# A recommendation tower on one core: one-hot results evicted in pairs, id spreads by DMA, and the moves of one tile spread among Gram units

## The chip, the cores and the metric

The kernel runs on one core of a Trainium2 chip. The metric is the device time of one execution in microseconds, 122.56 us before the change (median of three runs, 122.13 to 122.66). The engines are named as the profile names them: PE is TensorE (PEld its weight load), DVE is VectorE, ACT is ScalarE, POOL is GpSimd, SP is SyncE. The source writes `scalar` for ACT and `vector` for DVE.

## The reference

A batch of 512 rows. Each row has a dense feature vector (128 numbers) and 26 ids; each id picks a row of 128 numbers from its own table. The 27 vectors of a row are multiplied pairwise, and the 351 products go with the dense vector, twice, into a small network.

```python
e = jnp.stack([tbl_0[ids[:, 0]], ..., tbl_25[ids[:, 25]]], axis=1)            # 512 x 26 x 128
combined = jnp.concatenate([dense[:, None, :], e], axis=1)                     # 512 x 27 x 128
interactions = jnp.einsum('bfd,bgd->bfg', combined, combined)                  # 27 x 27 per row
z = jnp.concatenate([dense, interactions[:, iu, ju]], axis=1)                  # upper triangle, 351
h = jnp.concatenate([z, dense], axis=1)                                        # 607
h = jnp.maximum(h @ W_top1 + b_top1, 0.0)                                      # 512
h = jnp.maximum(h @ W_top2 + b_top2, 0.0)                                      # 256
y = h @ W_top3                                                                 # 1
```

Ten of the 26 tables have 1000 rows; the others have 1250 to 125000.

## The kernel before, in words

All engines walk one list, `STEPS`, which `plan_steps` writes out by hand (L110 to L144). Each engine takes its own part of each step, in the order of the list, and waits on semaphores for the others. So the list sets the order on PE, DVE and ACT; SP and POOL have fixed orders of their own.

**One-hot stage.** The ten tables of 1000 rows are loaded whole (SP, L264) and looked up by a product. For table `i`, PE spreads its 512 ids over the partitions (`bcast`, L540): two products of 128x512, one into the PSUM region `gram[0]` that DVE reads, one into `gram[1]` that ACT reads. DVE and ACT then write the one-hot matrix in eight chunks of 128 rows (`mark`): in each half of four chunks DVE does three by a comparison (L460), ACT one by two activations (L396, L400). The table is split into two parts so that the product is exact enough: ACT rounds it (`cast`, L386) and DVE forms what is left (`low`, L452). PE multiplies, 16 products a table (`onehot`, L561), into one of four PSUM banks that are used in a ring (`RING`). ACT copies each result bank into `xT` (L434), which holds for each batch row its 27 vectors plus five of them a second time (32 slots of 4 bytes side by side). The dense vectors are turned by PE (`dense`, L549) and copied by ACT three times: into `denseT` and into two slots that are not neighbours.

**Gathered tables.** The other 16 tables are fetched row by row by POOL: 64 indirect DMAs (L305), 16 for each of four batch tiles of 128 rows, in groups of four. After some groups POOL waits until the first three gathers of a group have landed. For each group PE does four transposes (`group`, L572) and ACT or DVE copies the bank into `xT`.

**Tail.** For each batch tile PE forms the pairwise products four batch rows at a time (`gram`, L587), in four units of eight, which alternate between the regions `gram[0]` and `gram[1]`. Each unit is staged: ACT copies one half of the columns (L410), DVE overlays the others through masks (L473, L476). After the fourth unit the *moves*, eight copies of 32x96 on ACT (L417) and eight on DVE (L484), bring the staged products into `pairs`. Then come the first layer in two halves (L601, L603), ACT and DVE each taking one half out of PSUM, the second layer (L615), and on DVE the third (L502, L506). A last product turns the 512 results into rows (L620).

PE, before the first real product, runs transposes that only keep it busy: `WARM_UP` (L528) and `FILL` (L545).

## Time and profile before

| what | us |
|---|---|
| median of the runs (three) | 122.56 |
| the profiled execution itself | 122.37 |
| its span | 120.6 |
| PE busy (685 products) | 111.4 |
| DVE busy | 79.6 |
| ACT busy | 71.7 |
| POOL busy | 67.2 |
| last one-hot product ends at | 57.8 |
| last gather issued at | 93.0 |

The span is the time from the first to the last instruction in the profile; the execution's own time is 1.77 us longer. PE's granted clock is 1.00 of full speed in every stretch. A busy time of PE is not PE at its peak, because products are pipelined; where the start times of neighbouring rows tell more than the durations, they are used. In the chain of waits each piece starts where the one before it ends.

### The profile page before, as it was taken

How to read it: one execution, taken by the hardware profiler on the slowest of the kernel's cores; microseconds unless marked ns; L12 is line 12 of the kernel's file. 1: busy time of each engine (PE TensorE's matmuls, PEld its weight loads, DVE VectorE, ACT ScalarE, POOL GpSimd, SP SyncE). 2: the span in 40 equal slices, each digit the busy share in tenths (PEclk: the TensorE clock that was granted, in tenths of full speed). 3: DMA queues.
4: the chain of work that ended last, by engine and by line, in shares of the span. 5: the costliest groups of instructions: out<-in, count | busy, mean ns of one | idle time of the engine just before them, and what ended most of it. 6: DMA issues, size and time to landing. Idle time of an engine off the chain costs nothing.

```text
span 120.6 us, 1879 instructions
## 1 busy us (share of the span) xinstructions
PE 111.4 (92%) x685; PEld 94.1 (78%) x685; DVE 79.6 (66%) x128; ACT 71.7 (59%) x132; POOL 67.2 (56%) x72
## 2 busy tenths in 40 slices
PE   4979999999999999999799949999999879998981
PEld 4647776866867768688699949989999769998960
DVE  1359999999999999991035762892439822564231
ACT  0399499999999999994531641680336522255200
POOL 3777477747688688677767477767767100000000
PEclk9999999999999999999999999999999999999999
DMA  3993755270643978212111112112211100000000
GB/s 64 389 370 115 232 203 177 84 222 23 217 137 126 235 285 302 56 44 58 50 44 50 45 50 60 45 44 63 52 44 49 38 0 5 0 0 0 0 0 1
DMA packets 4964, 11.99 MB, mean 99 GB/s; under 512 B 1742, under 2 KB 2002, under 8 KB 4956
## 3 DMA queue, kind: packets, MB, share of 16 engines
q1 hardware_dynamic: 2888, 7.67, 19.0%
q0 software_dynamic: 2048, 4.20, 12.3%
q8 instruction: 5, 0.08, 0.3%
q10 hardware_dynamic: 20, 0.02, 0.1%
q14 instruction: 3, 0.02, 0.1%
HBM read 11.88 MB, written 0.00 MB: 99 GB/s over the span
## 4 chain that ended last, share of the span: by engine, by line
PE 80%; ACT 11%; DVE 4%; issue 2%; POOL 0%; POOLq 0%; ACTq 0%; DVEq 0%
PE bank L561 32%; PE gram L587 21%; PE bank L615 6%; PE bank L572 6%; PE gram L540 5%; ACT pairs L417 5%; PE bank L603 4%; ACT xT L434 2%; DVE stage L473 2%; PE bank L528 2%; PE bank L601 2%; ACT stage L410 2%; ACT L396 1%; DVE stage L476 1%; DVE parts L452 1%
## 5 line engine op out<-in xcount | busy, mean ns | idle before, releaser
L305 POOL DMA_INDIRECT gath<-in_tbl,idx x64 | 66.3, 1036 | 26.0 <-issue 16.2
L561 PE MATMUL bank<-onehot,parts 128*128 128x512 f32 x160 | 41.0, 411 | 0.7 <-DVE parts L452 0.7
L561 PEld LDWEIGHTS bank<-onehot,parts 128*128 128x128 f32 x160 | 30.7, 197 | 8.0 <-issue 1.7
L460 DVE TENSOR_TENSOR onehot<-gram,row 128x1536 fp32r<-128x1536 f32 x20 | 34.6, 1746 | 2.1 <-PE gram L540 2.1
L587 PE MATMUL gram<-xT 128*128 128x108 f32 x256 | 29.5, 276 | 3.0 <-DVE stage L476 1.6
L587 PEld LDWEIGHTS gram<-xT 128*128 128x128 f32 x256 | 29.0, 192 | 3.7 <-ACT xT L434 1.9
L473 DVE COPY_PREDICATED stage<-overlaid,gram 128x384 f32<-128x384 int32 x16 | 9.3, 582 | 22.6 <-ACT stage L410 22.6
L434 ACT COPY xT<-bank 128x512 f32<-128x512 f32 x22 | 19.5, 920 | 5.4 <-PE bank L572 3.1
L410 ACT COPY stage<-gram 128x384 f32<-128x384 f32 x16 | 7.6, 480 | 22.5 <-PE gram L587 22.5
L396 ACT ACTIVATE distance<-gram,minus_row 128x512 f32<-128x512 f32 x20 | 13.6, 678 | 0.0
L452 DVE TENSOR_TENSOR parts<-table,parts 128x1024 fp32r<-128x1024 f32 (+1 forms) x11 | 12.3, 1117 | 1.6 <-ACT parts L386 1.6
L603 PE MATMUL bank<-pairs,wp 128*128 128x128 f32 x96 | 13.3, 275 | 0.0
L400 ACT ACTIVATE onehot<-distance 128x512 fp32r<-128x512 f32 x20 | 12.6, 632 | 0.6
L603 PEld LDWEIGHTS bank<-pairs,wp 128*128 128x128 f32 x96 | 12.0, 192 | 0.0
L386 ACT CAST parts<-table 128x1024 fp32r<-128x1024 f32 (+1 forms) x11 | 10.5, 961 | 1.6 <-PE bank L561 1.6
L417 ACT COPY pairs<-stage 32x96 f32<-32x96 f32 x32 | 8.6, 268 | 4.2 <-DVE stage L476 3.9
L572 PE MATMUL bank<-ident,gath 128*128 128x128 f32 x64 | 9.5, 279 | 0.5 <-ACT xT L434 0.5
L572 PEld LDWEIGHTS bank<-ident,gath 128*128 128x128 f32 x64 | 7.1, 141 | 3.4 <-issue 2.2
L540 PE MATMUL gram<-ids_r,pick 10*128 10x512 f32 x20 | 8.2, 493 | 0.0
L484 DVE COPY pairs<-stage 32x96 f32<-32x96 f32 x32 | 7.8, 243 | 0.6
L615 PE MATMUL bank<-w_sb,h1T 128*128 128x256 f32 x32 | 7.7, 385 | 0.0
L601 PE MATMUL bank<-denseT,wd 128*128 128x128 f32 x32 | 6.3, 278 | 0.4 <-ACT pairs L417 0.4
(32 smaller groups left out, 47.8 us busy)
## 6 DMA issues: line engine op xcount, KB each, us to landing
table<-in_tbl SPq DMA_DIRECT2D x10, 512.0 KB, 3.3
gath<-in_tbl,idx POOLq DMA_INDIRECT x64, 2.6
wp<-in_w_pairs SPq DMA_DIRECT2D x1, 768.0 KB, 7.1
w_sb<-in_w SPq DMA_DIRECT2D x1, 512.0 KB, 7.6
dense_sb<-in_dense SPq DMA_DIRECT2D x1, 256.0 KB, 4.7
wd<-in_w_dense_a SPq DMA_DIRECT2D x1, 256.0 KB, 6.0
wd<-in_w_dense_b SPq DMA_DIRECT2D x1, 256.0 KB, 6.7
b_bc<-in_b SPq DMA_DIRECT2D x1, 128.0 KB, 7.5
```

What stands on the lines that cost most here:

```text
L305: nc.gpsimd.indirect_dma_start(gath[:, t % GATHER_TILES, s, :], None, tables[GATHERED[s]], bass.IndirectOffsetOnAxis(idx[:, t * TABLES + G ...
L396: nc.scalar.activation(distance[:, n % 2, :], bcast_bank(i, "scalar"), ACT.Abs, bias=minus_row[:, c:c + 1]).then_inc(distance_ready, 1)
L417: last = nc.scalar.copy(dst, src)
L434: last = nc.scalar.copy(dst, src)
L452: nc.vector.tensor_tensor(parts[:, i % 2, 1, c], table[:, i % 3, c], parts[:, i % 2, 0, c].bitcast(F32), ALU.subtract).then_inc(parts_read ...
L460: nc.vector.tensor_tensor(onehot[:, i % 2, c, :], bcast_bank(i, "vector").unsqueeze(1).broadcast_to([P, len(chunks), BATCH]), row[:, c].un ...
L540: last = nc.tensor.matmul(bcast_bank(i, engine), pick[:, i:i + 1].broadcast_to([NOH, P]), ids_r[:], start=True, stop=True)
L561: last = nc.tensor.matmul(dst[:], parts[:, i % 2, part, c * DIM:(c + 1) * DIM], onehot[:, i % 2, c, :], start=(c == 0 and part == 0), stop ...
L572: last = nc.tensor.transpose(dst[:, n * P:(n + 1) * P], gath[:, t % GATHER_TILES, slot, :], ident[:])
L587: last = nc.tensor.matmul(gram[region][:, q, 0:4 * FEATURES], quad, quad[:, :, 0:FEATURES], start=True, stop=True)
L603: last = nc.tensor.matmul(to, wp[:, r, h], pairs[:, t % 2, r, :], start=False, stop=(r == BLOCKS - 1))
L615: last = nc.tensor.matmul(dst[:, 0:H2], h1T[:, t % 2, c, :], w2_sb[:, c, :], start=(c == 0), stop=(c == H1 // P - 1))
```

## The change

The batch rows of a tile are renumbered on the host (ids and dense alike), so that a result bank is copied in the order in which `xT` lies. Then:

- **Pairs.** Two one-hot results lie in two neighbouring banks, and one ACT copy (`pair`) takes both, two neighbouring slots at a time: 128x512x2 elements. The last pair is split, half of the batch on ACT, half on DVE (`pair_rest`).
- **Dense.** The dense vectors come by DMA already turned (`denseT`, `dense_qj`); one ACT copy writes them into two neighbouring slots. PE's four transposes and three ACT copies go.
- **Ids.** ACT's spread of ids for tables 2 to 9 comes by DMA (`spread_ids`, 256 KB written each), in SP's queue. PE does one spread product a table instead of two. The spreads of tables 0 and 1 are done at once, before `FILL`; `WARM_UP` goes from 9 to 7. ACT loads its function table at the very start (a one-column activation), and its first cast goes ahead of its first mark.
- **Groups.** Only tile 0's four groups stand in the one-hot stage, in banks of the region `gram[1]`, and ACT copies them. Tile 1's four groups stand between the first Gram units. The last tile is gathered into `table`, which is free by then, and its last group is copied in two halves (`group_rest`).
- **Tail.** `moves` is a step of its own: tile 0's moves stand between tile 1's Gram units in three pieces, tile 1's and 2's after their units, tile 3's after its own. `sum`, the DVE addition for the dense weights, moves from the one-hot stage to behind tile 0's Gram units. Tile 2's first layer stands ahead of tile 3's Gram units, around the last group; tile 2's second layer behind them.

The core of the diff:

```diff
-GROUPS = [list(range(g, min(g + GROUP, NG))) for g in range(0, NG, GROUP)]
+GROUPS = [list(range(g, g + GROUP)) for g in (NG - GROUP, *range(0, NG - GROUP, GROUP))]
 RING = 4
-GROUP_BEHIND = {1: 1, 2: 1, 3: 1, 4: 1, 6: 1, 7: 1, 8: 1, 9: 1}
-WARM_UP = 9
+GROUP_BEHIND = {1: 1, 3: 1, 5: 1, 7: 1}
+WARM_UP = 7
 HALVES = 2
 SPREAD_REGION = {"vector": 0, "scalar": 1}
...
-    steps = [("bcast", 0), ("mark", 0, 0), ("cast", 0, 0), ("low", 0, 0), ("mark", 0, 1), ("cast", 0, 1), ("low", 0, 1)]
-    steps += [("cast", 1, 0), ("bcast", 1), ("mark", 1, 0), ("low", 1, 0), ("mark", 1, 1)]
+    steps = [("bcast", 0), ("bcast", 1), ("fill",), ("cast", 0, 0), ("mark", 0, 0), ("low", 0, 0), ("cast", 0, 1), ("mark", 0, 1), ("low", 0, 1)]
+    steps += [("cast", 1, 0), ("mark", 1, 0), ("low", 1, 0), ("mark", 1, 1)]
...
-    steps += take(1, 2 * len(GROUPS)) + grams(0) + grams(1)
-    steps += layer1(0) + take(2, 4) + [("layer2", 0)] + grams(2)
-    steps += take(3, 2) + layer1(1) + take(3, 1) + [("layer2", 1)] + take(3, 1) + grams(3)
-    steps += layer1(2) + [("layer1", 3, 0), ("layer2", 2), ("layer1", 3, 1), ("layer2", 3)]
-    return steps + [("turn",)]
+    steps += gram(0, 0) + take(2) + gram(0, 1) + take(1) + gram(0, 2) + take(1) + gram(0, 3) + [("sum",)]
+    steps += gram(1, 0) + moves(0, [0, 1]) + gram(1, 1) + moves(0, [2]) + gram(1, 2) + moves(0, [3]) + gram(1, 3)
+    steps += moves(1) + layer1(0) + take(4) + [("layer2", 0)] + grams(2)
+    steps += take(2) + moves(2) + layer1(1) + take(1) + [("layer2", 1), ("layer1", 2, 0)] + take(1)
+    steps += [("group_rest", *steps[-1][1:]), ("layer1", 2, 1)] + grams(3) + moves(3)
+    return steps + [("layer2", 2)] + layer1(3) + [("layer2", 3), ("turn",)]
...
+            def spread_ids(i):
+                if i >= SCALAR_SPREADS + 2:
+                    sp.wait_ge(onehots_ready["scalar"], HALVES * SCALAR_CHUNKS * (i - 1))
+                sp.dma_start(ids_bc[:, i % 2, :], ids_rows[i:i + 1, :].broadcast_to([P, BATCH])
+                             ).then_inc(ids_bc_loaded[i], 16)
+
             load_table(0)
             load_table(1)
-            sp.dma_start(dense_sb[:], dense).then_inc(dense_loaded, 16)
+            spread_ids(2)
             load_table(2)
+            sp.dma_start(dense_qj[:], dense_qj_t).then_inc(dense_qj_loaded, 16)
+            for i in range(3, NOH):
+                load_table(i)
+                spread_ids(i)
+            sp.dma_start(denseT[:], dense_t).then_inc(denseT_loaded, 16)
             sp.dma_start(wd[:, 0, :], w_dense_a).then_inc(wd_loaded, 16)
             sp.dma_start(wd[:, 1, :], w_dense_b).then_inc(wd_loaded, 16)
-            for i in range(3, NOH):
-                load_table(i)
             sp.dma_start(overlaid[:], masks).then_inc(masks_loaded, 16)
             sp.dma_start(wp[:], w_pairs).then_inc(wp_loaded, 16)
...
+        def pair_slots(s, first_tile, tiles):
+
+            first = 2 * s[1]
+            n = slice(first_tile * P, (first_tile + tiles) * P)
+            return (xT[:, first_tile:first_tile + tiles, :, :, first:first + 2].rearrange("p t q j s -> p (t q j) s"),
...
+                elif s[0] == "dense":
+                    act.wait_ge(dense_qj_loaded, 16)
+                    nc.scalar.copy(xT[:, :, :, :, DENSE_SLOT:DENSE_SLOT + 2].rearrange("p t q j s -> p (t q j) s"),
+                                   dense_qj[:].unsqueeze(2).broadcast_to([P, BATCH, 2])).then_inc(freed["scalar"], 1)
+                elif s[0] == "pair":
+                    act.wait_ge(bank_full, USE[("onehot", 2 * s[1] + 1)] + 1)
+                    dst, src = pair_slots(s, 0, TILES // 2 if s == LAST_PAIR else TILES)
+                    nc.scalar.copy(dst, src).then_inc(freed["scalar"], 1)
```

On ACT, one table of the one-hot stage, with a group's copy behind it. Before (a cast, the copy of a result, two marks, a group's copy); `bank2` and `bank3` are result banks:

```order
L386 CAST parts<-table 128x1024 [waits bank_full,table_loaded5]
L434 COPY xT<-bank2 128x4x4x32 [waits bank_full]
L396 ACTIVATE distance<-gram1,minus_row 128x512 [waits onehots_by_scalar,bcast_full]
L400 ACTIVATE onehot<-distance 128x512 [waits distance_ready]
L396 ACTIVATE distance<-gram1,minus_row 128x512 [waits onehots_by_scalar]
L400 ACTIVATE onehot<-distance 128x512 [waits distance_ready]
L434 COPY xT<-bank3 128x128x4 [waits bank_full]
```

Now, for a table with a pair:

```order
L464 CAST parts<-table 128x1024 [waits bank_full,table_loaded7]
L521 COPY xT<-bank0 128x512x2 [waits bank_full]
L477 ACTIVATE distance<-ids_bc,minus_row 128x512 [waits onehots_by_scalar,ids_bc_loaded7]
L481 ACTIVATE onehot<-distance 128x512 [waits distance_ready]
L477 ACTIVATE distance<-ids_bc,minus_row 128x512 [waits onehots_by_scalar]
L481 ACTIVATE onehot<-distance 128x512 [waits distance_ready]
L524 COPY xT<-gram1 128x128x4 [waits bank_full]
```

The copy of a result is twice as long and comes with every second table; the ids are read from `ids_bc`, and ACT waits for a DMA there, not for PE; the group's bank lies in `gram1`.

On PE, from the end of the one-hot stage into the Gram units. Before (tile 0's units; all groups of tiles 0 and 1 are done):

```order
L587 MATMUL gram0<-xT 128x108 [waits freed_by_vector,freed_by_scalar]
L587 MATMUL gram0<-xT 128x108 x7
L587 MATMUL gram1<-xT 128x108 x8
L587 MATMUL gram0<-xT 128x108 [waits staged]
L587 MATMUL gram0<-xT 128x108 x7
L587 MATMUL gram1<-xT 128x108 [waits staged]
L587 MATMUL gram1<-xT 128x108 x7
L587 MATMUL gram0<-xT 128x108 [waits staged,freed_by_vector,freed_by_scalar]
L587 MATMUL gram0<-xT 128x108 x7
L587 MATMUL gram1<-xT 128x108 [waits staged]
```

Now tile 1's groups (`gath`) stand between tile 0's units:

```order
L692 MATMUL gram0<-xT 128x108 [waits freed_by_scalar]
L692 MATMUL gram0<-xT 128x108 x7
L680 MATMUL bank1<-ident,gath 128x128 [waits last_row_in1_0,rows_in1_0,freed_by_scalar]
L680 MATMUL bank1<-ident,gath 128x128 x3
L680 MATMUL bank1<-ident,gath 128x128 [waits last_row_in1_1,rows_in1_1,freed_by_scalar]
L680 MATMUL bank1<-ident,gath 128x128 x3
L692 MATMUL gram1<-xT 128x108 [waits freed_by_scalar]
L692 MATMUL gram1<-xT 128x108 x7
L680 MATMUL bank0<-ident,gath 128x128 [waits last_row_in1_2,rows_in1_2,freed_by_vector]
L680 MATMUL bank0<-ident,gath 128x128 x3
L692 MATMUL gram0<-xT 128x108 [waits staged,freed_by_scalar]
L692 MATMUL gram0<-xT 128x108 x7
```

The groups moved from the one-hot stage to here, and every unit has its own wait for the copies into `xT`.

On PE, from the last group of gathered rows (`rows_in3_3`). Before:

```order
L572 MATMUL bank0<-ident,gath 128x128 [waits rows_in3_3,last_row_in3_3,freed_by_vector,freed_by_scalar]
L572 MATMUL bank0<-ident,gath 128x128 x3
L587 MATMUL gram0<-xT 128x108 [waits staged,freed_by_vector,freed_by_scalar]
L587 MATMUL gram0<-xT 128x108 x7
L587 MATMUL gram1<-xT 128x108 [waits staged]
L587 MATMUL gram1<-xT 128x108 x7
L587 MATMUL gram0<-xT 128x108 [waits staged]
L587 MATMUL gram0<-xT 128x108 x7
L587 MATMUL gram1<-xT 128x108 [waits staged]
L587 MATMUL gram1<-xT 128x108 x7
L601 MATMUL bank1<-denseT,wd 128x128 [waits moved_by_scalar,moved_by_vector,freed_by_vector,freed_by_scalar]
```

Now:

```order
L680 MATMUL bank0<-ident,table 128x128 [waits last_row_in3_3,rows_in3_3,freed_by_vector]
L680 MATMUL bank0<-ident,table 128x128 x3
L706 MATMUL bank0<-denseT,wd 128x128 [waits moved_by_vector,moved_by_scalar,freed_by_vector]
L708 MATMUL bank0<-pairs,wp 128x128 x3
L706 MATMUL bank0<-denseT,wd 128x128
L708 MATMUL bank0<-pairs,wp 128x128 x3
L692 MATMUL gram0<-xT 128x108 [waits staged,freed_by_vector,freed_by_scalar]
L692 MATMUL gram0<-xT 128x108 x7
```

and, two units later:

```order
L692 MATMUL gram1<-xT 128x108 [waits staged,freed_by_vector,freed_by_scalar]
L692 MATMUL gram1<-xT 128x108 x7
L720 MATMUL bank1<-w2_sb,h1T 128x256 [waits freed_by_scalar,freed_by_vector]
L720 MATMUL bank1<-w2_sb,h1T 128x256
L720 MATMUL bank1<-w2_sb,h1T 128x256 [waits freed_by_vector]
L720 MATMUL bank1<-w2_sb,h1T 128x256
L706 MATMUL bank1<-denseT,wd 128x128 [waits moved_by_vector,moved_by_scalar,freed_by_scalar]
L708 MATMUL bank1<-pairs,wp 128x128 x3
```

Half a first layer (of tile 2) now stands between the last group and the Gram units of tile 3, and a second layer alone, where before there were a whole first layer and more, between those units and the first layer of tile 3.

## Rows read from the trace of the kernel before

**Rows 1.** The page: busy times; the gathers (busy, mean ns); table loads (median us to landing).

```profile
PE 111.4 (92%) x685; PEld 94.1 (78%) x685; DVE 79.6 (66%) x128; ACT 71.7 (59%) x132; POOL 67.2 (56%) x72
...
L305 POOL DMA_INDIRECT gath<-in_tbl,idx x64 | 66.3, 1036 | 26.0 <-issue 16.2
...
table<-in_tbl SPq DMA_DIRECT2D x10, 512.0 KB, 3.3
```

**Rows 2.** Chain of waits, start and one-hot stage: start us, us, what.

```profile
1.52 2.18 PE bank L528 x9
...
4.94 1.28 ACT L396
...
20.96 3.66 PE bank L561 x16
24.62 0.65 PE gram L540 x2
```

**Rows 3.** Timeline of TensorE, first one-hot product: start us, us, instructions [idle before].

```profile
8.98 5.84 PE L561 MATMUL bank<-onehot,parts 128*128 128x512 f32 x16 [0.65 <-DVE parts L452]
```

**Rows 4.** Timeline of VectorE, one-hot stage and one block of moves.

```profile
17.19 1.22 DVE L452 TENSOR_TENSOR parts<-table,parts 128x1024 fp32r<-128x1024 f32 x1
...
19.98 0.68 DVE L515 TENSOR_TENSOR wd<-wd 128x512 f32<-128x512 f32 x1
...
33.86 3.40 DVE L460 TENSOR_TENSOR onehot<-gram,row 128x1536 fp32r<-128x1536 f32 x2
...
38.33 3.44 DVE L460 TENSOR_TENSOR onehot<-gram,row 128x1536 fp32r<-128x1536 f32 x2
...
91.40 2.03 DVE L484 COPY pairs<-stage 32x96 f32<-32x96 f32 x8
```

**Rows 5.** Timeline of ScalarE, one table of the one-hot stage.

```profile
30.68 1.04 ACT L386 CAST parts<-table 128x1024 fp32r<-128x1024 f32 x1
31.62 1.09 ACT L434 COPY xT<-bank 128x512 f32<-128x512 f32 x1
32.49 0.69 ACT L396 ACTIVATE distance<-gram,minus_row 128x512 f32<-128x512 f32 x1
...
34.99 0.70 ACT L434 COPY xT<-bank 128x512 f32<-128x512 f32 x1
```

**Rows 6.** Timeline of GpSimd, three of its 64 gathers.

```profile
17.27 1.94 POOL L305 DMA_INDIRECT gath<-in_tbl,idx  x1 [0.30 <-issue]
...
87.76 0.94 POOL L305 DMA_INDIRECT gath<-in_tbl,idx  x1 [0.30 <-issue]
...
93.02 0.95 POOL L305 DMA_INDIRECT gath<-in_tbl,idx  x1 [0.30 <-issue]
```

**Rows 7.** DMA issues, 92 to 93.5 us: issues, median us to landing.

```profile
gath<-in_tbl,idx POOLq DMA_INDIRECT x2, 2.5
```

**Rows 8.** Timeline of TensorE, the unit that waited on moves.

```profile
71.43 3.82 PE L587 MATMUL gram<-xT 128*128 128x108 f32 x32 [1.57 <-DVE stage L476]
```

**Rows 9.** Chain of waits, from the first layer to the end.

```profile
76.16 0.22 PE bank L601 x2
76.38 0.67 PE bank L603 x6
...
78.84 1.90 PE bank L572 x16
...
82.75 7.14 PE gram L587 x64
...
98.45 7.41 PE gram L587 x64
...
109.84 0.46 PE bank L601 x2
...
115.38 1.85 PE bank L615 x8
...
118.70 0.26 ACT y_rows L429
```

More of the change, by code:

```diff
@@ L45 @@
 PARTS = 2
[L46 to L47 removed]
+SLOT_FEATURE = [1 + t for t in ONEHOT] + [1 + t for t in GATHERED] + [0]
+DENSE_SLOT = FEATURES - 1
+AGAIN = [DENSE_SLOT] + [DENSE_SLOT - 4 + g for g in range(4)]
 SLOTS = FEATURES + len(AGAIN)
@@ L126, in plan_steps @@
         if n < NOH:
-            steps += [("cast", n, 0), ("onehot", i), ("bcast", n), ("mark", n, 0), ("low", n, 0), ("mark", n, 1)]
-        else:
-            steps.append(("onehot", i))
+            steps.append(("cast", n, 0))
+        steps.append(("onehot", i))
+        if i % 2:
+            steps.append(("pair", i // 2))
+        if i == NOH - 1:
+            steps.append(("pair_rest", i // 2))
+        if n < NOH:
+            steps += [("bcast", n), ("mark", n, 0), ("low", n, 0), ("mark", n, 1)]
@@ L130, in plan_steps, with gram, moves @@
         if i == 0:
             steps.append(("dense",))
-        steps += take(TILES, GROUP_BEHIND.get(i, 0))
+        steps += take(GROUP_BEHIND.get(i, 0))
+    def gram(t, u):
+        return [("gram", t, u)]
     def grams(t):
         return [("gram", t, u) for u in range(len(UNITS))]
+    def moves(t, parts=range(4)):
+        return [("moves", t, j) for j in parts]
     def layer1(t):
         return [("layer1", t, 0), ("layer1", t, 1)]
-    steps += take(1, 2 * len(GROUPS)) + grams(0) + grams(1)
@@ L164 @@
-USE, EMPTIED_BY = plan_ring()
-USES = sorted(USE, key=USE.get)
-def emptied(engine, last_use):
-    return sum(EMPTIED_BY[s] == engine for s in USES[:last_use + 1])
-def build(nc, dense, masks, ids_cols, ids_rows, tables, w_pairs, w_dense_a, w_dense_b, b1, w2, b2, w3, out):
+    steps += gram(0, 0) + take(2) + gram(0, 1) + take(1) + gram(0, 2) + take(1) + gram(0, 3) + [("sum",)]
+    steps += gram(1, 0) + moves(0, [0, 1]) + gram(1, 1) + moves(0, [2]) + gram(1, 2) + moves(0, [3]) + gram(1, 3)
+    steps += moves(1) + layer1(0) + take(4) + [("layer2", 0)] + grams(2)
@@ new lines, in evicted_by @@
+def evicted_by(s):
+    if s[0] == "pair_rest":
+        return ("vector",)
+    if s[0] in ("dense", "pair", "group_rest", "turn"):
+        return ("scalar",)
+    if s[0] == "group":
+        return ("vector",) if s[1] > 1 and s[2] in (0, 2) else ("scalar",)
+    if s[0] == "layer1":
+        return ("vector",) if s[2] == 1 else ("scalar",)
+    return ("vector",) if s[0] == "layer2" else ()
+EVICTIONS = {engine: [s for s in STEPS if engine in evicted_by(s)] for engine in ("scalar", "vector")}
@@ new lines, in evictions_until, with early_group, plan_banks @@
+def evictions_until(engine, s):
+    return EVICTIONS[engine].index(s) + 1
+def early_group(s):
+    return s[0] == "group" and s[1] == 0
+def plan_banks():
+    bank_of, ring = {}, 0
+    for s in USES:
+        if early_group(s):
+            bank_of[s] = ("early", s[2] % 2)
+        else:
+            bank_of[s] = ("ring", ring % RING)
+            ring += 1
+    emptied_by, holder = {}, {}
+    for s in USES:
+        if bank_of[s] in holder:
+            before = holder[bank_of[s]]
+            if before[0] == "onehot":
+                before = ("pair", before[1] // 2)
+            if before in (LAST_PAIR, LAST_GROUP):
+                before = (f"{before[0]}_rest", *before[1:])
+            emptied_by[s] = before
+        holder[bank_of[s]] = s
+    return bank_of, emptied_by
@@ L174, in build @@
+BANK_OF, FREED_WITH = plan_banks()
+def build(nc, dense_t, dense_qj_t, masks, ids_cols, ids_rows, tables, w_pairs, w_dense_a, w_dense_b, b1, w2, b2, w3, out):
     ctx = ExitStack()
@@ L254, in build, with gathered, bank_at @@
         block = ctx.enter_context(nc.Block())
+        def gathered(t, s):
+            if t < LATE_TILE:
+                return gath[:, t, s, :]
+            return table[:, s // CHUNKS, s % CHUNKS * DIM:(s % CHUNKS + 1) * DIM]
+        def bank_at(s):
+            where, n = BANK_OF[s]
+            if where == "ring":
+                return bank[n // 2][:, n % 2, :]
+            quads = BATCH // P
+            return gram[EARLY_REGION][:, n * quads:(n + 1) * quads, :].rearrange("p a b -> p (a b)")
         @block.sync
@@ L576, in _ @@
                     n = len(UNITS) * t + u
-                    if u == 0:
-                        wait_emptied(max(USE[x] for x in USE if x[0] in ("dense", "onehot") or
-                                         (x[0] == "group" and x[1] == t)))
+                    wait_slots(t, u)
                     first_quad, quads, region = UNITS[u]
```

204 lines of the change are left out of this document (110 added, 94 removed).

## The prediction

> **What bounds the kernel now.** I read the page first. Its busy line [rows 1] makes PE the fullest engine. The chain of waits then shows two regimes. Up to 57.8 us it is PE alone: a table's sixteen products take 3.66, the two id spreads ahead of them 0.65, a group's four transposes about 0.48 (sixteen take 1.90) [rows 2, 9]. The timelines of DVE and ACT show that this is nearly a tie. DVE repeats itself every 4.47 us (its marks begin at 33.86 and 38.33) [rows 4]; ACT, between 30.68 and 35.6, has 4.9 us of work for one table and a group [rows 5]; PE needs 3.66 + 0.65 + 0.48 = 4.8. Whoever speeds up one of the three must look at the other two. From 57.8 us the chain is PE with short handoffs: Gram units (7.14 us for a tile's four), first layer (0.89 a quarter), second layer (1.85), and gaps where units wait for moves (1.57 at 71.43) [rows 8, 9].
>
> The view that matters most for this change is POOL's timeline, which is in no chain. Its 64 gathers run one behind the other to the end: the last is issued at 93.02 and lands 2.5 us later, at 95.5 [rows 6, 7]. PE takes them up only about 97: the Gram units behind begin at 98.45 [rows 9], and 0.48 of transposes and a copy of 0.70 lie between. So before, POOL has about 1.5 us to spare, and a change that brings PE forward by more than that runs into the gathers.
>
> **The change part by part.** All sums are against the profiled execution: 122.37 us, of which 120.6 are span, 0.2 below the median of 122.56.
>
> *Start.* Two transposes fewer at 0.24 each (2.18 for nine) [rows 2]: 0.48 sooner. The spreads and FILL before the first product are only reordered. PE then waited 0.65 for DVE's first remainder [rows 3]. That wait came from ACT: its function-table load of 1.28 at 4.94 [rows 2], then both activations ahead of the cast. Now the load runs during the DMAs and the cast is first. DVE begins at 4.46, marks for 1.7 and subtracts for half of 1.22 or a little more (6.9), while PE is still at its transposes; the wait goes. First product at 8.98 - 0.48 - 0.65 = 7.85; with 5.84 for the sixteen as before [rows 3] table 0 ends at 13.7 instead of 14.8. The loads could upset this: I assume that table 0 lands as before, since its place in SP's queue is the same.
>
> *One-hot stage, PE.* One spread instead of two saves one 512-column product at the stream's rate, 3.66/16 = 0.23, so 0.42 a table. Dense transposes go (0.48). Four groups instead of eight stand here: 1.9 us leaves, and is paid in the tail. PE needs 3.66 + 0.42 + half of 0.48 = 4.3 a table.
>
> *DVE.* Its group copies and `sum` (0.68) [rows 4] leave the stage; two marks and a remainder stay, 4.47 a table. That is now more than PE's 4.3, so DVE is next in line. From the spread of table 2 at 13.7 + 0.42 = 14.1, eight tables take 35.8: 49.9, and PE's last half table 1.83 more: 51.7.
>
> *ACT.* Its single-slot copy takes 1.09 for 512 elements, a group copy (four slots at a time) 0.70 [rows 5]. No row shows two at a time. From below: the cast, 1024 elements side by side, 1.04 [rows 5]; from above: two single copies, 2.18. Two group copies would be 1.40; a pair has twice the runs, so I take 1.5, of which about 0.1 overlaps. From 13.7 on ACT has eight casts at 0.94, sixteen marks at 1.25 (32.49 to 34.99 for two) [rows 5], four pairs and dense at 1.4, four group copies at 0.6, ahead of the last mark: 7.5 + 20.0 + 7.0 + 2.4 = 36.9, to 50.6, and 1.83 for PE: 52.4. So ACT, not DVE, is last, by 0.7, and the stage ends at 52.4 instead of 57.8. At 1.04 a pair DVE rules (51.7); at 2.18 it is 52.4 + 5 x 0.7 = 55.9.
>
> *Ids by DMA.* ACT waits for them; behind the wait stand its two marks, and PE waits for those. They are issued when the marks two tables earlier are done, some 6 us ahead, and a load of twice the bytes lands in 3.3 [rows 1], so I count nothing. In SP's queue each stands ahead of the next table, which is needed some 8 us later; nothing again. If one came 3 us late, it would cost that much of the slack below. ACT's reading them from SBUF I take at the 0.69 of now.
>
> *Tail, as far as PE decides.* The first unit waits for ACT's half pair, between 0.70 and 1.09, say 0.85: 53.25. Then eight units 14.3, tile 1's groups 1.9, first layer 3.57, four groups 1.9, second layer 1.85, tile 2's units 7.14, two groups 0.95, first layer 3.57: 88.4 at group 2 of tile 3. The 1.57 that units waited for moves is gone: with two pieces between units, ACT has 0.5 for staging and at most 1.1 of moves in a unit's 1.79. Behind it 0.48, second layer 1.85, half a first layer 1.79: 92.55 at the last group.
>
> *The gathers.* Group 2 lands at 87.76 + 2.5 = 90.3, the last group at 95.5 [rows 6, 7]. So PE waits 1.9 at the one and then reaches the other at 94.4, where it waits 1.1. These 3.0 us are what the one-hot stage won and cannot keep; they also are a cushion: the stage may end at 55.4 without changing the end. I leave the gather stream where it is: same 64 issues, same queue, same eleven remainders on DVE. What sets its speed: 64 gathers at 1.036 mean [rows 1] against 0.95 undisturbed, 5.5 us of stretching. A gather that starts inside a remainder (17.27 in 17.19 to 18.41) takes 1.94 [rows 4, 6]. One that lies in DVE's moves (93.02, moves 91.40 to 93.43) takes 0.95. `sum` also takes two SBUF inputs; in the stage it fell between two gathers' starts, now it lies at about 63 us and may stretch one: bounds 0 and 0.99, I take 0, the row of now. Moves in pieces: 0 by the row.
>
> The Trainium skill (SBUF — State Buffer, section "SBUF: two separate sides") says that an fp32 copy from SBUF to SBUF on DVE locks GpSimd out, so that it cannot write descriptors. The row at 93.02 does not bear this out for copies of 32x96. By that rule, each of tile 0's separate pieces could hold up a gather of its own; this is the slower rival below.
>
> *From the last group on.* 95.5, transposes 0.48, half a first layer 1.79, units 7.14: 104.9. From the end of the units to the first layer it took 3.98 (98.45 + 7.41 to 109.84) for staging and moves [rows 9], and nothing here shortens that; PE fills it with a second layer only and idles some 2 us. 108.9. First layer: 109.84 to 115.38 less the second layer of 1.85 that lay in it, 3.7: 112.6. Last second layer to the end of ACT's last copy, 115.38 to 118.96, 3.6: 116.2. Output and frame as before, 122.37 - 118.96 = 3.4: 119.6. Carried to the median, 0.2 more: I forecast 119.8, a gain of 2.8 us, 2.2%.
>
> **The rivals.**
> *The gathers come sooner.* If the shorter stage catches fewer of them in a remainder, up to half of the 5.5 us goes. PE would reach the last group at 92.55 unhindered; the floor is 119.8 - 3.0 = 116.8. For it: the stretches depend on phase. Against: at 4.47 us a table DVE's phase to the gathers is the one it had. Likely 118.2.
> *ACT holds the stage.* Pairs at 2.18: the stage ends at 55.9, the first unit 0.3 later again, 0.8 over the cushion: 120.6; with late ids on top 121.5. For it: the single-slot copy is slow; against: group copies are not.
> *Nothing left.* Eight id spreads of 256 KB go into the same DMA engines as the gathers. At half of a table's 3.3 us or less each takes 0.7 to 1.6 of them; if POOL's four waits in the stage grow by 0.7 each, the stream ends 2.8 later: 122.6, no change.
> *Slower.* The pieces of moves (three) and `sum`, now alone among gathers, each hold one up by 0.99, and landings slip besides: 4.0 us on the stream, 123.8. Decides from 3.2 us of lateness; below that it is no loss.
>
> **How the numbers follow.** Forecast 58%, own range 118.9 to 120.8. Sooner gathers 16% (117 to 118.9), ACT 13% (120.6 to 121.7), nothing left 8%, slower 5%. The range of eight in ten takes most of the two neighbours: 117.8 to 121.8. A measurement of this kernel tells about 0.5% from no change, here 0.6 us. Faster 0.87, same 0.08, slower 0.05.
>
> **What would show it.** After: the first product at about 7.9 without a wait; DVE and ACT full, PE with small waits in the stage; its last product at 51.7 to 53; a pair's copy at 1.5; no wait for staging in tile 1's units; PE waiting for gathers at tile 3's groups 2 and 3, the last issued near 93; about 2 us of idle PE before the last first layer. The forecast is wrong if the last gather is issued before 91 or after 95, or if the stage ends behind 55.4.

## The result, and the profile after

The kernel after takes 119.61 us, median of five runs (119.07 to 121.9), against 122.56 for the kernel before in the same comparison (five runs, 122.13 to 124.79): a ratio of 0.976, 95% interval 0.973 to 0.979, so 2.9 us less. The forecast was 119.8. The profile below is of the slowest of the five executions, 121.9 us with a span of 120.1; the median one has no profile.

The page of the kernel after: busy us (share of the span) and instructions for each engine; then, in order, the granted clock in 40 slices, the head of the part on the chain that ended last, and the DMA issues of the one-hot tables with the median time to landing.

```profile
PE 108.2 (90%) x671; PEld 92.3 (77%) x671; DVE 77.6 (65%) x126; ACT 68.4 (57%) x131; POOL 64.8 (54%) x72
...
PEclk9999999999999999999999999999999999999999
...
POOL 37%; DMA 30%; issue 14%; PE 13%; ACT 2%; DVE 1%; DVEq 0%; ACTq 0%; POOLq 0%
...
table<-in_tbl SPq DMA_DIRECT2D x10, 512.0 KB, 5.1
```

PE is still the fullest engine, at 90%, but it has only 13% of the chain. In the kernel before the chain was mostly PE's from the one-hot stage to the end [rows 2, 9]; now 81% of it is POOL, the landings of its DMAs, and the time between their issues. An engine at 90% that does not set the time is what this profile has to teach. A table lands in 5.1 us instead of 3.3 [rows 1].

TensorE's timeline: start us, us, instructions [idle before <-releaser].

```profile
7.51 5.78 PE L669 MATMUL bank<-onehot,parts 128*128 128x512 f32 x16
13.22 0.49 PE L652 MATMUL gram<-ids_r,pick 10*128 10x512 f32 x1
13.65 3.92 PE L669 MATMUL bank<-onehot,parts 128*128 128x512 f32 x16
17.50 0.49 PE L652 MATMUL gram<-ids_r,pick 10*128 10x512 f32 x1
...
22.60 3.92 PE L669 MATMUL bank<-onehot,parts 128*128 128x512 f32 x16
...
45.20 7.53 PE L669 MATMUL bank<-onehot,parts 128*128 128x512 f32 x32
53.41 2.04 PE L692 MATMUL gram<-xT 128*128 128x108 f32 x16 [0.68 <-ACT xT L521]
...
60.57 9.10 PE L692 MATMUL gram<-xT 128*128 128x108 f32 x80
...
76.51 0.63 PE L680 MATMUL bank<-ident,gath 128*128 128x128 f32 x4 [1.41 <-DMA gath<-in_tbl,idx]
...
86.96 0.63 PE L680 MATMUL bank<-ident,table 128*128 128x128 f32 x4 [0.51 <-DMA table<-in_tbl,idx]
...
92.16 0.63 PE L680 MATMUL bank<-ident,table 128*128 128x128 f32 x4 [1.00 <-DMA table<-in_tbl,idx]
...
97.67 0.63 PE L680 MATMUL bank<-ident,table 128*128 128x128 f32 x4 [1.36 <-DMA table<-in_tbl,idx]
...
99.92 7.30 PE L692 MATMUL gram<-xT 128*128 128x108 f32 x64
...
111.06 0.46 PE L706 MATMUL bank<-denseT,wd 128*128 128x128 f32 x2 [2.10 <-ACT pairs L500]
```

The wait of 0.65 ahead of the first product [rows 3] is gone. The last one-hot product ends at 52.7 (45.20 + 7.53) instead of 57.8. The 80 products at 60.57 run through without the 1.57 that units had waited [rows 8]. Then PE waits four times for a gather, 4.3 us together, and once, for 2.1, with nothing to do before the last first layer. So PE came forward by 5 us and gave most of it back at the gathers.

GpSimd's timeline: the four gathers of tiles 0 and 1 before which POOL waited (14.14, 26.95, 41.33, 54.15), two that were stretched (29.44, 47.14), three around DVE's `sum` and moves (63.23 to 66.06), and the last one:

```profile
14.14 0.94 POOL L378 DMA_INDIRECT gath<-in_tbl,idx  x1 [1.33 <-DMA gath<-in_tbl,idx]
...
26.95 0.94 POOL L378 DMA_INDIRECT gath<-in_tbl,idx  x1 [2.53 <-DMA gath<-in_tbl,idx]
...
29.44 1.51 POOL L378 DMA_INDIRECT gath<-in_tbl,idx  x1 [0.30 <-issue]
...
41.33 0.94 POOL L378 DMA_INDIRECT gath<-in_tbl,idx  x1 [3.42 <-DMA gath<-in_tbl,idx]
...
47.14 1.66 POOL L378 DMA_INDIRECT gath<-in_tbl,idx  x1 [0.30 <-issue]
...
54.15 0.94 POOL L378 DMA_INDIRECT gath<-in_tbl,idx  x1 [1.59 <-DMA gath<-in_tbl,idx]
...
63.23 0.94 POOL L378 DMA_INDIRECT gath<-in_tbl,idx  x1 [0.30 <-issue]
64.81 0.94 POOL L378 DMA_INDIRECT gath<-in_tbl,idx  x1 [0.63 <-DMA gath<-in_tbl,idx]
66.06 0.95 POOL L378 DMA_INDIRECT gath<-in_tbl,idx  x1 [0.30 <-issue]
...
94.96 0.94 POOL L378 DMA_INDIRECT table<-in_tbl,idx  x1 [0.30 <-issue]
```

The four waits are 8.9 us together; at the same four places the kernel before has three, of 1.61, 1.60 and 0.64, which is 3.85. Against that, five gathers are stretched here instead of nine. The last gather is issued at 94.96, 1.9 later than before [rows 6]. From there to the end it is 26.94 (121.9 - 94.96), and in a second profiled execution 26.93 (below). By that distance the median run would issue its last gather at about 92.7; this is an estimate, not a row.

### The profile page after: what moved, and what is told of

Same layout as the page of the kernel before. It is cut to its first block, busy times and chain, and to the rows that moved or that the text cites. A ratio compares the mean times of both kernels' runs of the same rounds, so it can differ in the third digit from the quotient of the medians.

```text
span 120.1 us, 1841 instructions
## 1 busy us (share of the span) xinstructions
PE 108.2 (90%) x671; PEld 92.3 (77%) x671; DVE 77.6 (65%) x126; ACT 68.4 (57%) x131; POOL 64.8 (54%) x72
## 4 chain that ended last, share of the span: by engine, by line
POOL 37%; DMA 30%; issue 14%; PE 13%; ACT 2%; DVE 1%; DVEq 0%; ACTq 0%; POOLq 0%
POOL gath L378 30%; DMA gath<-in_tbl,idx 20%; DMA table<-in_tbl,idx 9%; POOL table L378 7%; PE gram L692 6%; PE bank L708 3%; DMA idx<-in_ids_cols 2%; ACT pairs L500 2%; PE bank L720 2%; PE bank L706 1%; PE bank L680 1%; DVE stage L568 0%; ACT stage L491 0%; DVE h L600 0%; DVE h2w L604 0%
## 5 line engine op out<-in xcount | busy, mean ns | idle before, releaser
L378 POOL DMA_INDIRECT gath<-in_tbl,idx x48 | 48.9, 1019 | 24.3 <-issue 12.2
L378 POOL DMA_INDIRECT table<-in_tbl,idx x16 | 15.1, 943 | 6.0 <-issue 3.7
L477 ACT ACTIVATE distance<-ids_bc,minus_row 128x512 f32<-128x512 int32 x16 | 11.4, 715 | 0.0
L591 DVE TENSOR_SCALAR h1T<-bank,b_sb 128x128 f32<-128x128 f32 x8 | 2.4, 347 | 9.2 <-PE bank L708 9.2
L524 ACT COPY xT<-bank 128x512 f32<-128x512 f32 (+1 forms) x9 | 4.9, 573 | 5.0 <-PE bank L680 5.0
L706 PEld LDWEIGHTS bank<-denseT,wd 128*128 128x128 f32 x32 | 4.9, 191 | 3.0 <-issue 2.9
```

The costliest lines, as they stand in the source:

```text
L378: nc.gpsimd.indirect_dma_start(gathered(t, s), None, tables[GATHERED[s]], bass.IndirectOffsetOnAxis(idx[:, t * TABLES + GATHERED[s]:t * TA ...
L477: nc.scalar.activation(distance[:, n % 2, :], scalar_ids(i), ACT.Abs, bias=minus_row[:, c:c + 1]).then_inc(distance_ready, 1)
L706: nc.tensor.matmul(to, wd[:, 2, h], denseT[:, t * P:(t + 1) * P], start=True, stop=False)
```

## The experiments

What had to be told apart: does the gather stream set the time (my theory), or PE, or ACT? And which part of the change is worth what? Times are medians; before stands at 122.38 to 122.60 in these comparisons, so a ratio is the safer comparison of two kernels that did not run beside each other. Where a mean granted clock is given for an execution, 1.00 is full speed. Two parts of the change get a price of their own, the pairs (experiment 7) and the pieces of moves (experiment 9); no run prices the dense vectors, the place of the groups, or PE's spread products that the DMAs replaced.

### 1. The kernel as it is, once more

> The changed kernel as it is. Theory (the gather stream sets the end): 119.3 to 119.7 us, the last gather issued at 92 to 93.5 where the profiled execution on record (121.9) issued it at 94.96; time minus the issue of the last gather is the same in both, about 27 us. Rival (the 121.9 came from elsewhere, say a slower TensorE): the last gather is issued at about 95 again, or the difference of the two is not constant. Stage end (last one-hot product) 52.7 by both.

121.07 us (six runs, 119.28 to 123.71), ratio 0.980 [0.975, 0.986], which is more than the 119.3 to 119.7 that I expected. The profiled one took 121.32, its last gather at 94.39 and not at 92 to 93.5. What came as the theory had it is the distance from there to the end, 26.93.

The runs spread over 4.4 us. Part of that is TensorE's clock: the two longest (123.53 and 123.71) had a mean granted clock of 0.97, the four others (119.28 to 121.32) of 1.00. But at that full clock this kernel spreads over 2.0 us, and the one of experiment 5, in which POOL and PE wait for no gather, over 0.2 (four executions, 116.23 to 116.41). Times that hang on landings scatter.

### 2. Eight transposes more before the first product

```diff
-FILL = 10
+FILL = 18
```

> FILL is 18 instead of 10: eight transposes more before the first product, 1.9 us at 0.24. Theory (gather stream sets the end, PE has a cushion of 2.5 to 3 us): the last one-hot product ends 1.5 to 1.9 us later (at about 54.4), the waits for tile 3's groups shrink by as much, the time stays within 0.3 us of the changed kernel's. Rival (PE's chain sets the end, the waits are incidental): the time grows by 1.5 to 1.9 us.

122.5 us (twelve runs), ratio 1.000 [0.997, 1.004]. TensorE's timeline at the start, first the kernel as it is, then with `FILL` at 18:

```profile
7.26 5.23 PE L669 MATMUL bank<-onehot,parts 128*128 128x512 f32 x16
```

```profile
8.96 3.92 PE L669 MATMUL bank<-onehot,parts 128*128 128x512 f32 x16
```

The first product comes 1.7 later, but the sixteen take 3.92 instead of 5.23, and the first Gram unit is only 0.4 later (53.01 against 52.61). By PE alone at most 0.4 would be lost. The time rose by 1.4 at the median, and in the profiled pair by 2.2 (123.5 - 121.32): its last gather is 1.85 later (96.24), behind a wait of 3.71 in the stage and one of 2.36 at 87. The rest is TensorE's clock, behind one of its waits for a gather:

```profile
93.65 0.63 PE L680 MATMUL bank<-ident,table 128*128 128x128 f32 x4 [2.14 <-DMA table<-in_tbl,idx]
94.12 3.38 PE L720 MATMUL bank<-w_sb,h1T 128*128 128x256 f32 x8
```

The eight products take 3.38 here and 1.89 in experiment 1; the granted clock from 94 to 97 us is 0.56. So PE takes up the last group at 99.31, without a wait and about 0.4 later than the gather alone would have it. Seven of the twelve executions had a mean clock of 0.972 to 0.986; the five at 0.997 or more took 121.81 to 122.03, against 119.28 to 121.32 in experiment 1, so the clock is not the main part. The time followed the gathers, but my number missed: I had taken the stream as fixed, and it moved by 2 us. Why it moved is not shown. The wait of 3.71 falls among loads of tables; the one of 2.36 comes at 87 us, when only gathers are under way.

### 3. Fewer of POOL's waits

```diff
-SHORT_RUNS_FROM = 2
+SHORT_RUNS_FROM = TILES
```

> GpSimd waits for landed gathers after every second group in tiles 2 and 3 too, not after each: four of its pauses go. Theory (gather stream sets the end): each pause is 0.55 to 0.7 us, so the last gather is issued 1.8 to 2.6 us sooner and the time falls by as much, to about 117.3. The floor by PE's own chain is 116.8. Rival (PE sets the end): no change, 119.5. Third way: the queue is the limit and not the issuing, then landings take longer by what the pauses gave, and nothing is won.

119.93 us (six runs), ratio 0.975 [0.969, 0.981]. The last gather is issued at 91.45, 2.9 earlier than in experiment 1, and the median falls by 1.1 only, not to the 117.3 that I expected. In the profiled execution the rest went into TensorE's clock:

```profile
107.49 0.68 PE L706 MATMUL bank<-denseT,wd 128*128 128x128 f32 x2 [2.09 <-ACT pairs L500]
107.96 1.49 PE L708 MATMUL bank<-pairs,wp 128*128 128x128 f32 x6
```

Six products take 1.49 here and 0.83 in the experiments without it: after the pause of 2.09 the engine came back at 1.2 GHz (granted clock 0.53 from 107.4 to 110 us). That cost 1.6 us: from the start of this first layer to the last product of all it takes 8.34 here (107.49 to 115.83) and 6.73 in the kernel after (111.06 to 117.79). Four of the six executions had a mean clock of 0.984 to 0.986; the two at full clock took 118.49 and 119.92.

### 4. No id spreads by DMA

The edit leaves out the spreads for tables 4 to 9; ACT's marks for these tables read the ids of table 2 or 3 instead.

```diff
+                if i >= SCALAR_SPREADS + 2:
+                    return
...
-                            act.wait_ge(ids_bc_loaded[i], 16)
+                            act.wait_ge(ids_bc_loaded[SCALAR_SPREADS + i % 2], 16)
```

> The spreads of ids by DMA for tables 4 to 9 are left out (ScalarE's marks for these tables read the ids of tables 2 and 3, so its share of their one-hot matrices is another one): six DMAs of 256 KB fewer, and nothing else. Theory (they slow the gathers' landings in the one-hot stage, and with them the stream that sets the end): GpSimd's waits at the ends of its runs in the stage fall from 1.3 to 3.4 us each to 0.3 to 1.6, the last gather is issued 1 to 2.5 us sooner, the time falls by 0.8 to 2.2 us. Rival (the DMA engines have room, the id spreads cost nothing): within 0.4 us of the changed kernel.

121.5 us (seven runs), ratio 0.991 [0.987, 0.995]: no faster than experiment 1, where a fall by 0.8 to 2.2 was expected. The gathers issued between 17 and 53 us of the span, first in the kernel as it is, then without the spreads: issues, median us to landing.

```profile
gath<-in_tbl,idx POOLq DMA_INDIRECT x23, 4.5
```

```profile
gath<-in_tbl,idx POOLq DMA_INDIRECT x23, 3.2
```

With the spreads the median landing of a gather is 1.3 us longer. Yet POOL's four chances to wait in the stage give 1.39, 0, 4.00 and 1.38, together 6.8, against 5.9 in experiment 1. What counts is how long the few gathers take behind which POOL waits: the wait of 4.00 is for one issued at 35.47 that landed 5.93 later.

The edit did more than the expectation says. In SP's queue a spread waits for ACT's marks; without these waits the loads behind the tables start 5 us earlier. SP's issue of the largest one (the weights of the pairs, 768 KB), first in the kernel as it is, then without the spreads:

```profile
41.83 0.44 SPq L349 DMA_DIRECT2D wp<-in_w_pairs  x1
```

```profile
36.66 0.43 SPq L351 DMA_DIRECT2D wp<-in_w_pairs  x1
```

So the long wait lies among loads that the kernel as it is has later, and this experiment does not price the spreads. It shows that POOL's waits do not follow the median landing. That they hang on which gathers meet which loads fits this row and is not tested; why a single landing is as long as it is stays open.

### 5. POOL waits for the group before, not for the one just issued

```diff
-                    if t >= SHORT_RUNS_FROM or g % 2:
-                        pool.wait_ge(rows_in[t][g], 16 * (len(group) - 1))
+                    if t or g:
+                        at, ag = (t, g - 1) if g else (t - 1, len(GROUPS) - 1)
+                        pool.wait_ge(rows_in[at][ag], 16 * (len(GROUPS[ag]) - 1))
```

> GpSimd, after each group of four gathers, waits for the group before it and not for the one just issued; never more gathers are under way than before. Theory (the pauses of the gather stream set the end): its waits of 0.5 to 3.4 us go nearly all, the last gather is issued at 87 to 89 (64 at 1.25 from 2.9 on, plus stretches of 5), PE no longer waits for tile 3's groups by more than 0.3, and the time is PE's own: 116.6 to 117.4, plus up to 1.6 where TensorE comes back slow from the 2.1 us of idling ahead of the last first layer, as it did in the run with shorter pauses (its next three quarters took 3.46 instead of 2.7). Rival (PE sets the end, or DMA bandwidth does): the time stays at 119.5 to 121.

116.37 us (six runs, 116.23 to 118.27), ratio 0.949 [0.944, 0.954]. The head of the chain that ended last, and GpSimd's last gather:

```profile
PE 89%; DVE 4%; ACT 3%; issue 1%; POOL 0%; POOLq 0%; DVEq 0%; ACTq 0%
```

```profile
87.64 0.94 POOL L378 DMA_INDIRECT table<-in_tbl,idx  x1 [0.30 <-issue]
```

No gather is waited for any more, by POOL or PE, and the chain is PE's again. One wait condition on an engine that has 0% of the chain of the kernel before is worth 3.3 us by the ratios (0.976 against 0.949 of 122.5) and 4.7 by the medians of experiments 1 and 5. Two of the six executions took 118.2, at a mean clock of 0.985; the four at 1.00 took 116.2 to 116.4. So the clock can fall here too, though it did not in the profiled one.

### 6. The same wait in the kernel before

> The kernel before the change, with the same lagged waits on GpSimd. Theory (before the change PE's chain set the end, and the gathers had about 1.5 us to spare): no change within 0.3 us of 122.4, though the last gather is issued 4 to 6 us sooner. Rival (gathers set the end of both kernels): faster by 1 us or more.

122.74 us (twelve runs), ratio 1.002 [0.998, 1.005]. The last gather is issued at 87.68 instead of 93.02, and TensorE's waits stay what they were, as the one for the moves [rows 8]:

```profile
71.20 3.82 PE L588 MATMUL gram<-xT 128*128 128x108 f32 x32 [1.57 <-DVE stage L477]
```

That settles it: the kernel before was bound by PE and its handoffs, and its gathers had room; the kernel after is bound by the gathers. Freed of them, the change is worth 122.74 - 116.37 = 6.4 us and not 2.9.

### 7. Pairs as two copies of one slot, on the kernel of experiment 5

```diff
-                    nc.scalar.copy(dst, src).then_inc(freed["scalar"], 1)
+                    nc.scalar.copy(dst[:, :, 0:1], src[:, :, 0:1])
+                    nc.scalar.copy(dst[:, :, 1:2], src[:, :, 1:2]).then_inc(freed["scalar"], 1)
```

> As the first of this call, but each pair is evicted as two copies of one slot each, as before the change (the renumbered rows kept). Theory (ScalarE is within 0.5 us a table of being the bound): a single copy takes 0.6 to 1.1; if it is the stride between slots that made 1.09, two take 2.0 where a pair takes 1.09: 0.9 x 4 = 3.6 us more on ScalarE, whose waits in the stage are about 1.5; the stage ends 1.5 to 2.5 later, the time grows by as much over the first of this call. Rival (what made 1.09 was the old numbering's 512-byte stride; with the rows in order a single costs 0.65): two take 1.2, nothing changes.

120.12 us (seven runs), ratio 0.965 [0.959, 0.972], 3.8 more than experiment 5 by the medians. The clock is in that number: five executions had a mean of 0.984 to 0.986, and the two at 1.00 took 118.21 and 118.35, which is about 2 more than experiment 5 at full clock. ScalarE's timeline, the two copies; and, for the kernel after, a cast and one copy of a pair:

```profile
27.24 1.11 ACT L522 COPY xT<-bank 128x512 f32<-128x512 f32 x1
28.11 1.20 ACT L523 COPY xT<-bank 128x512 f32<-128x512 f32 x1
```

```profile
26.88 1.04 ACT L464 CAST parts<-table 128x1024 fp32r<-128x1024 f32 x1
27.83 1.08 ACT L521 COPY xT<-bank 128x1024 f32<-128x1024 f32 x1
```

A copy of 512 elements into one slot costs as much as one of 1024 into two neighbouring slots, and that costs what the cast of 1024 to contiguous addresses does. The batch rows are renumbered here, and a single copy is no faster than the 1.09 of the kernel before [rows 5], so the old numbering did not make it slow. With singles ACT holds the stage: it has 37% of the chain, and the first Gram unit starts at 54.26 instead of 52.54. The profiled executions lie 3.3 apart: 1.7 are that, and 1.6 a first layer at TensorE's low clock after the pause, as in experiment 3 (107.73, six products in 1.49).

### 8. Half of tile 2's first layer behind tile 3's Gram units

The edit, on the kernel of experiment 5:

```diff
-    steps += [("group_rest", *steps[-1][1:]), ("layer1", 2, 1)] + grams(3) + moves(3)
+    steps += [("group_rest", *steps[-1][1:]), *grams(3), *moves(3, [0, 1]), ("layer1", 2, 1), *moves(3, [2, 3])]
```

> As the one before, and the second half of tile 2's first layer moves from ahead of tile 3's Gram units into the pause behind them (between the moves). Theory: the 1.79 us fill the pause of 2.1; of these 0.4 come back as a wait for the last group's copy and 0.1 in the moves. 1.2 to 1.4 us below the kernel before it in this call, 115.4 to 116.1, and the slow comeback of TensorE's clock goes too, so the times scatter less. Rival (the pause ends when VectorE and ScalarE are done, and the added eviction on VectorE makes it longer by as much): 0 to 0.3 us.

116.02 us (six runs, 115.73 to 117.15), ratio 0.948 [0.943, 0.953]. It is the fastest version, though not measurably faster than experiment 5; 1.2 to 1.4 less were expected. All six executions had a mean clock of 0.995 or more. The pause became a half first layer and a short wait:

```profile
100.84 0.40 PE L707 MATMUL bank<-denseT,wd 128*128 128x128 f32 x2
...
104.23 1.13 PE L721 MATMUL bank<-w_sb,h1T 128*128 128x256 f32 x4 [0.56 <-DVE h1T L592]
105.37 0.46 PE L707 MATMUL bank<-denseT,wd 128*128 128x128 f32 x2
```

The last first layer starts at 105.37 against 105.58, although this execution's first sixteen products took 5.45 and those of experiment 5 took 4.54, and so its Gram units began 0.3 later. That is a gain of 0.5. Of the 1.79 that were moved, 0.54 came back as a wait for the last group's copy ahead of tile 3's units, and 0.5 between these units and the last first layer (4.35 against 3.83), where VectorE takes out the added half among its moves; the second of these is what the expectation's rival had.

### 9. Tile 0's moves in one block again

On the kernel of experiment 8. (A first attempt at experiments 9 and 10 ran on another chip. ACT stood still for 32 us ahead of the cast of one table there, the two kernels took 178.0 and 179.6, and the kernel before 154.7 instead of 122.5, so it tells nothing.)

```diff
-    steps += gram(0, 0) + take(2) + gram(0, 1) + take(1) + gram(0, 2) + take(1) + gram(0, 3) + [("sum",)]
-    steps += gram(1, 0) + moves(0, [0, 1]) + gram(1, 1) + moves(0, [2]) + gram(1, 2) + moves(0, [3]) + gram(1, 3)
+    steps += gram(0, 0) + take(2) + gram(0, 1) + take(1) + gram(0, 2) + take(1) + gram(0, 3) + moves(0) + [("sum",)]
+    steps += gram(1, 0) + gram(1, 1) + gram(1, 2) + gram(1, 3)
```

> The kernel with tile 0's moves in one block again (POOL waits a group later, tail reordered), on another chip: where it ran first, the loads of some tables came tens of us late, in this kernel and in the kernel before alike, so nothing could be read from its times. Theory: tile 1's third unit waits for its region until both engines have done the moves, 1.57 us as in the kernel before, and as PE sets the end here, the time grows by that and by up to 0.7 for the DVE addition behind the block: 117.6 to 118.3 against 116.0 without the edit. Rival: PE's wait is made up elsewhere (at the copies it waits for anyway, or the late groups): 116.0 to 116.4.

118.71 us (six runs, 117.08 to 119.24), ratio 0.961 [0.955, 0.968], somewhat more than the 117.6 to 118.3 expected. TensorE's timeline:

```profile
66.74 5.42 PE L693 MATMUL gram<-xT 128*128 128x108 f32 x32 [1.66 <-DVE stage L572]
```

and its windows from 62 to 72 us of the span (us, busy time and count of PE, PEld, DVE, ACT and POOL, granted clock, DMA share, GB/s), here and in experiment 8:

```profile
62.00:72.00 10.00, 8.34 (x60) 8.20 (x59) 5.91 (x17) 3.50 (x12) 7.56 (x9) 0.83 0.22 56
```

```profile
62.00:72.00 10.00, 9.68 (x87) 9.54 (x86) 8.06 (x25) 5.88 (x19) 7.55 (x9) 1.00 0.22 55
```

The wait is the 1.57 of before, a little longer. But the 32 products behind it take 5.42, which in the kernel before took 3.82 [rows 8]: TensorE came back from the wait at its low clock, 0.83 of full speed over the ten microseconds, and that costs 1.6 more. Two of the six runs took 117.1, at a mean clock of 0.996, and three 118.7, at 0.985. So the block itself costs about 1 us, the clock behind it 1.6 in the executions in which it falls.

### 10. `FILL` at 18 on the kernel of experiment 8

> The same base with FILL at 18 instead of 10, on another chip, for the same reason. Theory: PE sets the end, so the time follows the end of table 0's products: about 12.9 us instead of 12.7 to 13.0; 116.2 to 116.4 against 116.0, within the uncertainty. Rival: in most executions the slow first products (3.9 to 5.8 us for sixteen) cost more than eight transposes: then 115.5, with less spread from run to run.

116.55 us (six runs, 116.02 to 117.3), ratio 0.951 [0.947, 0.956], the same as experiment 8 within the intervals. The first product is at 8.89, sixteen take 3.90, the first Gram unit starts at 52.91 against 52.82. The extra transposes buy exactly the time that they take. With no gather to wait for, the 1.4 us of experiment 2 are gone, so they were not the transposes'.

## Why the prediction was right, and where it was not

**Start.** First product without a wait at 7.5 (7.25 to 7.61 in the eight profiles with `FILL` at 10; predicted 7.85), sixteen in 5.78, table 0 done at 13.2 (13.7). Right.

**One-hot stage.** Predicted to 52.4, measured 52.7. Two of its terms were mis-sized and cancelled. PE's table was put at 3.66 + 0.42 + half of 0.48 = 4.3; from start to start it is 4.28 without a group (13.22 to 17.50) and 4.68 with one (17.50 to 22.18), 4.48 on average. The pair: 1.09 where I chose 1.5 between 1.04 and 2.18, so the lower bound was the truth; group copies 0.58 instead of 0.70. So ACT is not last by 0.7. All three engines come to the same: PE 8.95 for two tables (13.65 to 22.60), ACT 8.96 (17.92 to 26.88), and DVE 4.46 a table. Equal periods alone don't tell who sets them, but in the profile of experiment 5 the chain through the whole stage, 7.61 to 51.9 us, is PE without a wait. So the step that made ACT the last one and DVE the next was wrong; PE is last, at 4.48 a table and not 4.3. DVE's marks:

```profile
25.59 3.41 DVE L555 TENSOR_TENSOR onehot<-gram,row 128x1536 fp32r<-128x1536 f32 x2
...
30.05 3.41 DVE L555 TENSOR_TENSOR onehot<-gram,row 128x1536 fp32r<-128x1536 f32 x2
```

The rival "ACT holds the stage" fell with the pair's 1.09, and experiment 7 shows what it would have been.

**Ids by DMA.** PE and ACT lost nothing, as said. But the rival "nothing left" was right in its first half: it had POOL's four waits grow by 2.8 together, and against the 3.85 of the kernel before they grew by 2.0 (experiment 1) and 5.0 (the kernel after). A part of that was given back by fewer stretches. How much of it the id spreads make, experiment 4 does not settle.

**Tail up to the gathers.** First unit at 53.41 (53.25), eight units and tile 1's groups without a wait for staging. Right. With the moves in one block the wait is back (experiment 9, 1.66); it costs about 1 us in time, and the clock can add 1.6.

**The gathers.** This is the step on which the forecast rested, and it held: POOL's stream sets the end (experiments 5 and 6), and PE waits at tile 3's groups 2 and 3. The sizes: 3.0 us were predicted for these two waits, 1.00 + 1.36 measured, and 1.41 + 0.51 at two earlier groups (tile 2's last, tile 3's second) that I had not in the sum. It is the same lateness, paid earlier: a stream that is behind at the end is behind at each group. The step that was stated wrongly is "I leave the gather stream where it is". It is no fixed quantity: 64 issues, five stretches here and eight in experiment 1 instead of nine, and waits in the stage of 5.9 to 8.9 us in three profiles with the same wait conditions (the kernel after, experiments 1 and 2), whose last gather is issued between 94.4 and 96.2. The value of 93.0 for the median was about right (92.7 by the distance to the end), and that was luck in part: fewer stretches and longer waits cancelled, and in experiment 1 the same kernel has a median of 121.07, outside the forecast's own range of 118.9 to 120.8.

**The cushion.** 3.0 us by the prediction. With the gathers out of the way on both sides the change brings 6.4 (experiments 5 and 6), with them 2.9: they hold back 3.5.

**Slower by the moves' pieces and `sum`.** Not seen in this profile: DVE's moves at 65.63 (1.00 long), 67.55 and 69.33 leave the gathers in them at 0.94 to 0.95, and no gather begins in `sum` (63.83 to 64.52). In four other profiles one does: it took 1.22 in experiment 3, 1.04 in 10, and 0.94 to 0.95 in 8 and 9. The Trainium skill ("SBUF — State Buffer", section "SBUF: two separate sides") says that an fp32 copy from SBUF to SBUF on DVE keeps GpSimd from writing descriptors. For copies of 32x96 no gather here shows it (the one at 66.06, inside the moves at 65.63, took 0.95). The gathers that are stretched are those that begin in DVE's remainders of 128x1024 (the one at 29.44 in 28.92 to 30.13); that is read from their positions, and no run took the remainders away.

**From the last group on.** In the chain, from the landing of the last gather to the start of the Gram units 2.55 (97.54 to 100.09; predicted 2.27), units 7.15, then 3.82 to the first layer (3.98), PE idle for 2.1. Right. The distance as a whole, 26.94 from the last issue to the end of the execution, was 26.6 in the forecast (119.6 - 93.0).

## What to carry to other kernels

Before a stage is shortened, look at the engine that is in no chain and ask when its last result is needed: if its room is less than the gain, the gain ends there, and the next edit belongs to that engine's waits. A wait for what has just been issued costs a whole landing; a wait for the group before it cost nothing here, and still bounds what is in flight: nine gathers at most, as waits after every second group allow too, where a wait after each group allows five. Idle time of TensorE has a second price, since it may come back at half its clock (1.5 to 1.6 us each time here).

## What the hardware showed

- A strided copy on ACT does not go by elements: single slots of 4 bytes take 1.11 and 1.20 us for 512 elements, pairs of 8 bytes 1.08 for 1024, where a cast of 1024 to contiguous addresses takes 1.04 (no plain contiguous copy was timed), and four slots side by side 0.58 for 512. So only the single slot costs extra. The Trainium skill ("SBUF — State Buffer", section "Specifications (TRN2)") says that SBUF has lines of 16 bytes and wants two accesses in each for full bandwidth. The rows agree: one access a line is slow, two or four are not. By that rule the pair would have been put at the cast's 1.04, and not at 1.5.
- TensorE's first products run at half rate although the granted clock of the stretch is 1.00 in the records. Of the kernel after, products between 9.0 and 10.2 us, and between 11.8 and 12.9 (duration ns min/median/max, first and last start us):

```profile
L669 PE MATMUL bank<-onehot,parts x4: 628/628/628, 9.0 to 10.2; 128*128 128x512 f32 x4
```

```profile
L669 PE MATMUL bank<-onehot,parts x6: 388/389/395, 11.8 to 12.9; 128*128 128x512 f32 x6
```

  Four products start in 1.2 us of the one stretch, six in 1.1 us of the other. The rate doubled in the middle of the sixteen, between 10.2 and 11.8; in experiment 5 it had at 9, in experiment 2 about with the first product. That is why the sixteen take 3.9 to 5.8 us.
- GpSimd locks into step with DVE. When POOL does not wait, each remainder stretches exactly one gather to 1.66, two of 0.94 follow, and with 0.30 between them the three take 4.47 (33.57 to 38.04), DVE's time for a table. GpSimd's timeline in experiment 5:

```profile
33.57 1.66 POOL L378 DMA_INDIRECT gath<-in_tbl,idx  x1 [0.30 <-issue]
35.54 0.94 POOL L378 DMA_INDIRECT gath<-in_tbl,idx  x1 [0.31 <-issue]
36.79 0.94 POOL L378 DMA_INDIRECT gath<-in_tbl,idx  x1 [0.30 <-issue]
38.04 1.66 POOL L378 DMA_INDIRECT gath<-in_tbl,idx  x1 [0.30 <-issue]
```

- After a pause TensorE sometimes returned at 1.2 GHz and sometimes at 2.4. At 1.2: 1.66 us (experiment 9), 2.09 (experiments 3 and 7), 2.14 (experiment 2, its granted clock 0.56 from 94 to 97) and 2.73 (experiment 4, 0.59 from 77 to 81). At 2.4: 1.57 (the kernel before and experiment 6) and 2.09 to 2.10 (the kernel after, experiments 1 and 5, and the last pause of 2 and 4). So the length of the pause alone does not decide it; what does stays open.
